# Expert weights split two tiles ahead, and a second unread product on TensorE

## The reference

```
probs = softmax(h @ gate_w.T)                 # 2048 tokens, 64 experts
topk_w, topk_idx = top_k(probs, 6);  topk_w /= sum(topk_w)
hid = silu(einsum('th,eih->tei', h, experts_w1))   # 256 -> 176, per expert
y   = einsum('tei,ehi->teh', hid, experts_w2)      # 176 -> 256
routed = einsum('teh,te->th', y, combine)          # the six chosen experts
```

## Time and profile before

| what | us |
|---|---|
| median of 3 runs | 2077.67 (2066.0 to 2079.49) |
| the profiled execution, its own time | 2081.04 |
| its span, first to last instruction | 2079.3 |
| TensorE busy | 1650.1 (79%) |
| VectorE busy | 1341.5 (65%) |
| ScalarE busy | 929.4 (45%) |
| GpSimd busy | 671.5 (32%) |
| mean granted clock of TensorE | 0.842 of full speed |

### The profile page before, as it was taken

One profiled execution on the slowest core, in us unless ns is written; L12 is line 12 of the kernel. 1 busy time (PEld: TensorE's weight loads), 2 busy tenths in 40 slices (PEclk: granted clock), 3 DMA queues, 4 the chain that ended last, 5 costly groups with the idle time before them and its releaser, 6 DMA issues. The chain is left out here.

```text
span 2079.3 us, 33315 instructions
## 1 busy us (share of the span) xinstructions
PE 1650.1 (79%) x9324; PEld 1240.9 (60%) x9324; DVE 1341.5 (65%) x2125; ACT 929.4 (45%) x1696; POOL 671.5 (32%) x554
## 2 busy tenths in 40 slices
PE   7689996899968999689997853289987966667741
PEld 5466664666646666466665742278876865556630
DVE  3578885788867888678885532644455455555547
ACT  3455554555545555455553201044444455555510
POOL 0334343343433443343440075612222222222210
PEclk8799998999989999899997575655577599999955
DMA  3011220122201212012210043254454455555434
GB/s 128 0 53 61 67 61 0 53 61 65 63 0 51 62 61 66 2 45 67 62 55 3 19 164 136 96 152 132 134 148 146 133 151 172 160 164 142 132 129 161
DMA packets 140945, 185.01 MB, mean 89 GB/s; under 512 B 19241, under 2 KB 113463, under 8 KB 140736
## 3 DMA queue, kind: packets, MB, share of 16 engines
q1 hardware_dynamic: 128576, 158.65, 25.7%
q0 software_dynamic: 12288, 25.41, 3.5%
HBM read 147.85 MB, written 44.50 MB: 93 GB/s over the span
## 5 line engine op out<-in xcount | busy, mean ns | idle before, releaser
L976 DVE SCALAR_TENSOR_TENSOR e<-bank,scal,e 128x511 f32<-128x511 f32 (+2 forms) x384 | 287.3, 748 | 52.6 <-ACT e L767 17.3
L1368 POOL DMA_INDIRECT outputs<-hsw,x_rows x160 | 157.5, 985 | 499.3 <-DVE hsw L1264 471.9
L1322 POOL TENSOR_TENSOR ssq<-ssq,ysq 128x512 f32<-128x512 f32 x128 | 164.4, 1284 | 466.2 <-ACT ysq L772 466.2
L400 PE MATMUL bank<-hw_hi,ew_hi 128*88 128x128 f32 x640 | 188.7, 298 | 135.6 <-DVE ew_lo L888 135.6
L888 DVE TENSOR_TENSOR hid_lo_rows<-hid_rows,hid_hi_rows 88x256 fp32r<-88x256 f32 x160 | 67.4, 421 | 306.1 <-ACT hid_hi_rows L718 210.8
L400 PE MATMUL bank<-h_hi,wi_hi 128*128 x512 | 240.2, 469 | 19.5 <-POOL wi_lo L1309 14.6
L475 PE MATMUL bank<-e,wn 128*128 128x512 f32 x512 | 252.9, 617 | 0.0
L400 PEld LDWEIGHTS bank<-hw_hi,ew_hi 128*88 128x88 f32 x640 | 125.5, 196 | 184.5 <-DVE ew_lo L888 184.5
L402 PE MATMUL bank<-h_hi,wi_lo 128*128 x512 | 204.0, 398 | 0.0
L401 PE MATMUL bank<-h_lo,wi_hi 128*128 x512 | 203.9, 398 | 0.0
L767 ACT ACTIVATE e<-bank,scal 128x512 f32<-128x512 f32 x128 | 99.7, 779 | 203.1 <-PE bank L402 203.1
(11 more groups left out here) (245 smaller groups left out, 3853.8 us busy)
## 6 DMA issues: line engine op xcount, KB each, us to landing
ew<-expert_w SPq DMA_DIRECT2D x320, 176.0 KB
wi<-in_w SPq DMA_DIRECT2D x128, 256.0 KB, 2.7
x_rows<-grouped SPq DMA_DIRECT2D x160, 130.0 KB
wo<-out_w SPq DMA_DIRECT2D x128, 128.0 KB, 2.3
got<-outputs SPq DMA_DIRECT2D x16, 768.0 KB, 4.3
grouped<-zeros_out SPq DMA_DIRECT2D x65, 130.0 KB
outputs<-hsw,x_rows POOLq DMA_INDIRECT x160, 3.0
x_all<-x_t SPq DMA_DIRECT2D x4, 512.0 KB, 8.5
```

Source lines behind the costliest of these rows:

```text
L400: mm(out, w_hi, x_hi, start=first, stop=False)
L976: v.scalar_tensor_tensor(dst[:, d:], src[:, 0:SEQ - d], taps(TAPS - 1 - d), dst[:, d:], ALU.mult, ALU.add).then_inc(S[done], 1)
L1322: g_.tensor_tensor(ssq[:, :], ssq[:, :], ysq[:, :], ALU.add).then_inc(S["ssq_done"], 1)
L1368: g_.indirect_dma_start(outputs, bass.IndirectOffsetOnAxis(x_rows[:, i % XD, EMB:EMB + 1].bitcast(U32), 0), y_rows[:, i % YD, :], None, bo ...
```

## The change

ScalarE and VectorE make the halves of the weights for tile i + 2 in turn i, not for tile i + 1, and as the last work of the turn: on ScalarE behind the high half of the hidden values, on VectorE behind the low half of the hidden values and behind the copy of the result. Ahead of the loop the halves of tiles 0 and 1 are made instead of tile 0 alone. TensorE makes two unread products of 512 columns in each turn instead of one. Nothing else differs: neither the semaphores nor the buffers nor SyncE's and GpSimd's lists.

```diff
@@ tensor
                 first(i)
                 if i:
                     second(i - 1)
-                fill(1)
+                fill(2)
@@ scalar
             weights(0)
             rows_in(0)
             rows_in(1)
+            weights(1)
             for i in range(ETILES):
-                if i + 1 < ETILES:
-                    weights(i + 1)
                 if i + 2 < ETILES:
                     rows_in(i + 2)
...
                 high(hid_hi[0:IHALF, i % 2, :], hid[0:IHALF, i % 2, :]).then_inc(S["hid_hi"], 1)
+                if i + 2 < ETILES:
+                    weights(i + 2)
@@ vector
             rows_in(0)
             rows_in(1)
+            weights_low(1)
             for i in range(ETILES):
...
-                if i + 1 < ETILES:
-                    weights_low(i + 1)
                 if i:
                     row_done(i - 1)
+                if i + 2 < ETILES:
+                    weights_low(i + 2)
```

## The result

| | us |
|---|---|
| before, median of 4 runs | 2078.58 (2066.0 to 2097.93) |
| changed, median of 4 runs | 1832.8 (1830.29 to 1837.77) |
| ratio | 0.8838, 95% interval 0.8793 to 0.8884 |
| changed, profiled execution | 1833.51, span 1831.7 |

The changed kernel's runs lie within 0.5%.

What follows compares the result with a forecast made beforehand. TensorE's wait for the weights' low half, in a ring through three engines, bounds the high-clock turn; 160 turns of 2.45 us plus 4, 4 and 8 make 408 us instead of 637.9, so 1850 us, range 1825 to 1950.

Steps and rivals of the forecast that it cites:

- What bounds the kernel: Expert stage, 637.9 us: at the high clock TensorE waits only for the weights' low half, 76.8 us in 220.
- the ring: Expert stage before, high clock: a turn of 3.62 us is a ring of latencies through three engines, `ew_lo` taking 1.05.
- The turn: Changed expert stage at the high clock: TensorE's own work sets a turn of 2.45 us, ends at 2.41 and 2.62.
- The covers: TensorE's waits for `hid_lo` and `ew_lo` in the new turn: both done 0.85 us before they are needed.
- The sum: Expert stage: 160 x 2.45 = 392 us, plus 4, 4 and 8, makes 408 in place of 637.9; 1850 us in all.
- The second product: TensorE, each tile: costs 0.23 us at the high clock, 0.43 at the low; worth only fewer falls, faster returns of clock.
- T: Length of a turn by TensorE's own work: 1.78 + 0.46 + 0.21 = 2.45 us.
- SyncE: Rival, chance 0.14: SyncE's queue (2.22 us a tile) or transfers pace the stage, T 2.7 to 3.0, 1891 to 1939 us.
- the signs named for a wrong forecast: Changed profile: `ew_hi` waiting for the load, `ew_lo` or scatter longer, or long windows at clock 0.50 with 4.4 to 4.7 us turns.
- the margin of 1 us: Weights' loads, expert stage: 2.5 + 4.3 = 6.8 us needed against 7.8 available, so loads cost nothing.
- VectorE against GpSimd: Rival, chance 0.08: scatter and VectorE's weights and hidden work shut each other out, T = 2.7, 1891 us.
- The low clock: Rival, low clock stays, 4.6 us turns: chance 0.12 for part, still faster; 0.05 over 71% of stage; all tiles low 2179 us.

Runs made afterwards that it cites:

- e2: Kernel before with two unread products per tile instead of one, nothing else changed: 2012.49 us, ratio 0.9894 to before.
- e11: Changed kernel with one unread product and the copy of the result behind the low half of the weights again: 1811.51 us, ratio 0.8866 to before.
- e10: Changed kernel with one unread product per tile instead of two, measured in the third set: 1812.16 us, ratio 0.887 to before.
- e3: Changed kernel without any unread product: 1920.88 us, ratio 0.9446 to before.
- e9: The changed kernel itself, run again beside its variants in the third set: 1813.7 us, ratio 0.8876 to before.
- e1: Changed kernel with one unread product per tile instead of two, measured in the first set: 1812.46 us, ratio 0.892 to before.
- e4: Changed kernel, two unread products, with the copy of the result behind the low half of the weights again: 1817.77 us, ratio 0.8948 to before.
- e7: Changed kernel with one unread product and SyncE reading row and expert numbers for eight tiles at a time: 1886.64 us, ratio 0.9138 to before.
- e12: Changed kernel with one unread product and SyncE's reads made without comparison with the bounds: 1781.24 us, ratio 0.8716 to before.

## Why the prediction was right

It gave 1850 us, 1825 to 1950; measured were 1832.8.

**What bounds the kernel**: right. The wait named in the earlier trace rows went from 76.8 us in 220 to 3.2 in 320, and e2, which left the ring as it was, kept its 3.63 us. One line was misread: the `ew_hi` at 1704.96 is that of the tile after the one whose `ew_lo` starts at 1705.43, so `ew_lo` does not follow it; its own `ew_hi` had ended at 1702.25, a turn earlier. That ScalarE is in no hurry there is all the more true.

**What moved.** One step was put wrongly in words: I treated ScalarE's `weights` as moved. The high half of tile i + 2 as the last work of turn i, before the rows of turn i + 1, is where it already stood as the first work of turn i + 1; with tile 1 made ahead of the loop, ScalarE's list of instructions is the same from its first to its last. So the title and the section on the change say too much: ScalarE made its half two tiles ahead before. The change is VectorE's: `ew_lo` of the tile after next, in the place where `ew_lo` of the next one stood. The layout of the turn was made from the right order, so no number came of it. That the copy now stands ahead of `ew_lo` is worth nothing by itself (e11 against e10).

**The turn.** 2.45 us forecast from TensorE's own work, 2.38 measured in a turn without a wait. The products are 1.77 for 1.78, the unread ones 0.47 for 0.46; the transposes cost 0.14, less than my lower end of 0.17. The covers held, a little shorter than the 0.85 us worked out: the `hid_lo` of 1604.19 is done at 1604.61, and its reader, the second product, starts 1.00 us behind the first product of 1604.38, so 0.77 us later; the `ew_lo` of 1602.63 ends at 1603.69, 0.69 us before the first product of 1604.38, which reads it. That the mean turn of 2.44 us is so near to the 2.45 forecast is partly luck: the transposes were put 0.07 us too high, and the short waits put 0.04 us back.

**The sum.** 389.8 us for the stage instead of 408. Of the 18 us, 160 x 0.07 = 11 are the turn, and the 8 for stretches at the low clock were not needed: from 1380 to 1700 us the clock is 1.00. The additions for start, end and small delays, 8 us in all, stand against 389.8 - 381 = 9 us. A slip in a rival's sum changes nothing: with half of the tiles at the low clock, 564 us for the stage make 2081 - 637.9 + 564 = 2007 us, not 2013.

**The second product.** That its worth lies in the clock was right for the order before (e2, clock 0.99). For the new order it was not needed: with one product the clock is at 0.99 (e10), without any it falls to 0.50 for long stretches (e3). And its cost of 0.23 us in T was no cost, since SyncE paced beside TensorE. How the 248 us split depends on which part comes first. With the product first (e2), 0.36 us a tile or 57 us are the clock (3.99 to 3.63) and 1.19 us a tile or 191 us the ring (3.63 to 2.44). With the order first (e10 against e9), the order alone gives all of it, the high clock included, and the second product nothing.

**SyncE**: the term that was mis-sized. I worked out 2.22 us a tile and measured, where it never waits, 2.37 to 2.39 (e1, e10). A list of four was put at 8.9 us. In e10, from 1380 to 1700 us, the shortest list takes just that, 8.9 us, but the mean is 9.6: the step of 1.48 came from a place of the kernel before where nothing was in the way, while here single transfers take longer to issue than their 0.33 us now and then, and the gap of 3.48 is 3.6 us in the median.

```profile
1494.93 0.33 SPq L337 DMA_DIRECT2D ew<-expert_w  x1
1495.37 1.04 SPq L339 DMA_DIRECT2D ew<-expert_w  x1
```

Why a transfer at times takes longer, the runs do not show. So the rival was half true: SyncE and TensorE are equal within 0.02 us, and the first one to be relieved shows nothing. Two of the signs named for a wrong forecast are there, at a small size. One is the wait of `ew_hi` for the load: the margin of 1 us was used up at times, 15.2 us of waits in 320, behind which ScalarE's other work stood. The other is the longer scatter.

**VectorE against GpSimd**: half of the exclusion came, and the half that would have cost time did not. In the turn above the scatter starts at 1603.35, 0.34 us before `ew_lo` ends, and takes 1.20 instead of 0.98 us, while `ew_lo` takes 1.06 against 1.05. It ends 0.86 us behind `ew_lo` (1604.55 against 1603.69). So does the scatter of e4 shown above, which starts just behind the start of an `ew_lo` and takes 1.84 us: it ends 0.85 us behind it. In e10 all 132 scatters that start with more than 0.13 us of an `ew_lo` left end 0.86 to 0.87 us behind it. This is what a scatter that cannot go on before the subtraction ends would show. The other way round nothing is held: where the scatter begins first (14 times in the changed kernel) `ew_lo` keeps its 1.06 us, and the `hid_lo` of 1604.19 starts in the middle of a scatter. GpSimd had 1.2 us a turn to spare, so nothing of the time shows it. The rule of the Trainium skill (SBUF — State Buffer, the section on the two separate sides) names a VectorE operation with two SBUF inputs and a GpSimd operation that reads SBUF as excluding each other, and the scatters' lengthening agrees with it; that VectorE would have to wait where the scatter began first is what neither nor these turns show.

**The low clock**: it did not come with unread products, and e3 shows that the rival was real. By the rule of the Trainium skill (TensorE: Matmul & The Clock Gate, the part on the clock gate) the low clock is the default and activity of TensorE lifts it; e3's row, 100 of 100 us busy at 0.50, does not agree if busy time is taken for activity. Which property of the 512-column product makes the difference between e3 and e10 was not tested.

## What to carry to other kernels

When a turn is a ring of latencies through several engines, make what can be made early one turn earlier on the engine that makes it last, and lay out the whole new turn, with the queue that issues transfers as one of the engines: here it was the next bound, within 0.02 us of TensorE. A queue's own time should be taken from rows at the new rate or given a margin (here the mean was some 7% above the sum of the undisturbed steps), and it is relieved by less work per item, not by larger pieces, which are late all at once. An unread product is worth its place only by the clock: try one less after each change of the order, and look at the clock again where TensorE starts to wait for loads, as in e7.

## What the runs showed of the hardware that I had not expected

- SyncE's comparison of numbers with their bounds is dear: with it, reading eight numbers puts 3.5 to 3.7 us between two transfers (e10), without it 1.64 us (e12).
- TensorE busy for 100 of 100 us on matmuls of 128 and 256 columns, with 88 columns of weights or 88 rows, and transposes, stays at 0.50. With one more product per tile, of 512 columns and with 128 rows and columns of weights, the clock is at 0.99 though TensorE is busy for less (e3 and e10).
- A scatter of GpSimd that starts during the weights' subtraction on VectorE (both operands in SBUF) ends some 0.86 us behind it: it takes 1.20 us instead of 0.98 with 0.34 us of the subtraction left, 1.84 us with 0.99 left. The subtraction is not lengthened (1.06 us). In the changed kernel two scatters start within 0.04 us behind the subtraction's start: they keep 0.98 us, and the subtractions take 1.10 and 1.13 us.
